# Splitting the last store of a fused conditional-mix and LoRA-expert kernel over two DMA queues

## The reference, cut to what matters

```python
W = weights[condition]                                  # 64 x 32 x 32
y = jnp.einsum('bct,bcd->bdt', x, W)
result = jnp.einsum('bnd,od->bno', y, W_base) + b_base
logits = jnp.einsum('bnd,ed->bne', y, W_gate)
...                                                     # softmax, top 2 of 8, renormalized: route_w
h = jnp.einsum('bnd,erd->bner', y, A)
delta = jnp.einsum('bner,eor->bno', h * route_w[..., None], B)
out = x + result + delta
```

## Time and profile before

| what | us |
|---|---|
| median of three runs | 97.9 |
| lowest and highest of the three | 97.78, 98.39 |
| the profiled execution, its own time | 97.5 |
| span in the profile, first to last instruction | 95.7 |
| granted TensorE clock, mean | 1.00 of full speed |

### The profile page before, as it was taken

How to read it: one execution, slowest core, us unless ns; L and a number is a source line. 1 busy time by engine, 2 the same in 40 slices (tenths; PEclk the granted TensorE clock), 3 DMA queues, 4 the chain that set the end, 5 groups by cost and what they waited for, 6 DMA issues and landing times.

```text
span 95.7 us, 1847 instructions
## 1 busy us (share of the span) xinstructions
PE 90.5 (95%) x657; PEld 87.6 (92%) x657; DVE 65.6 (69%) x234; ACT 23.8 (25%) x56; POOL 16.1 (17%) x29
## 2 busy tenths in 40 slices
PE   5997998999999999999999999999999999999980
PEld 1387997999999999999999999999999999999970
DVE  3768957767586686767675866867676767668880
ACT  5138433130403131221304031311313040311300
POOL 4384303030303021030303030120300000000000
PEclk9999999999999999999999999999999999999999
DMA  0895483060606233140606051331607020302005
GB/s 13 252 335 218 173 265 124 9 219 9 219 7 147 79 132 101 73 153 0 226 7 219 7 188 38 115 115 52 176 8 219 0 110 0 116 0 110 0 10 209
DMA packets 6361, 10.65 MB, mean 111 GB/s; under 512 B 1009, under 2 KB 1617, under 8 KB 6353
## 3 DMA queue, kind: packets, MB, share of 16 engines
q1 hardware_dynamic: 5904, 10.32, 32.6%
q0 software_dynamic: 448, 0.23, 1.1%
HBM read 6.35 MB, written 4.19 MB: 110 GB/s over the span
## 4 chain that ended last, share of the span: by engine, by line
PE 81%; DMA 10%; DVE 2%; issue 1%; ACT 1%; POOL 0%; SPq 0%; DVEq 0%; POOLq 0%
PE main_ps L485 51%; PE y_ps L467 12%; PE main_ps L505 12%; DMA mixw<-cond_w,row_ids 5%; PE main_ps L571 3%; DMA b_raw<-b_lora 3%; DMA table<-cond_w 2%; PE hwT_ps L495 2%; PE y_ps L565 1%; ACT b_hi L297 1%; POOL table_split L238 0%; DVE x_sb L448 0%; SPq L195 0%; DVE hw L385 0%; DVEq L67 0%
## 5 line engine op out<-in xcount | busy, mean ns | idle before, releaser
L485 PE MATMUL main_ps<-w_lo,y_hi 128*128 128x320 f32 x120 | 28.8, 321 | 0.0
L485 PE MATMUL main_ps<-w_hi,y_hi 128*128 128x320 f32 x120 | 28.8, 320 | 0.0
L485 PE MATMUL main_ps<-w_hi,y_lo 128*128 128x320 f32 x120 | 27.4, 311 | 0.0
L242 POOL DMA_INDIRECT mixw<-cond_w,row_ids x14 | 13.7, 976 | 49.3 <-PE y_ps L467 48.6
L485 PEld LDWEIGHTS main_ps<-w_hi,y_lo 128*128 128x128 f32 x120 | 20.3, 188 | 0.0
L485 PEld LDWEIGHTS main_ps<-w_lo,y_hi 128*128 128x128 f32 x120 | 19.9, 189 | 0.1
L485 PEld LDWEIGHTS main_ps<-w_hi,y_hi 128*128 128x128 f32 x120 | 19.4, 190 | 0.0
L467 PE MATMUL y_ps<-mix,x_sb 128*128 128x128 f32 x124 | 16.6, 276 | 0.6 <-DMA x_sb<-x 0.5
L467 PEld LDWEIGHTS y_ps<-mix,x_sb 128*128 128x128 f32 x124 | 15.6, 191 | 0.8 <-issue 0.7
L275 ACT ACTIVATE second<-top 128x1 f32<-128x1 f32 x16 | 4.7, 296 | 44.3 <-DVE top L367 44.3
L407 DVE TENSOR_TENSOR x_sb<-main_ps,x_sb 128x512 f32<-128x512 f32 x15 | 10.4, 691 | 5.7 <-PE main_ps L505 5.7
(11 more groups left out here) (66 smaller groups left out, 77.8 us busy)
## 6 DMA issues: line engine op xcount, KB each, us to landing
x_sb<-x SPq DMA_DIRECT2D x16, 256.0 KB, 2.9
out<-x_sb SPq DMA_DIRECT2D x15, 256.0 KB, 2.0
w_raw<-w_all SPq DMA_DIRECT2D x4, 324.0 KB, 4.6
b_raw<-b_lora SPq DMA_DIRECT2D x1, 256.0 KB, 2.8
bias_sb<-bias SPq DMA_DIRECT2D x1, 256.0 KB, 4.5
out<-x_sb SPq DMA_DIRECT2D x2, 128.0 KB, 1.8
mixw<-cond_w,row_ids POOLq DMA_INDIRECT x14, 2.4
table<-cond_w SPq DMA_DIRECT2D x1, 64.0 KB, 2.0
```

What stands on the lines that cost most here:

```text
L242: pool.indirect_dma_start(mixw[:, t, :], None, cond_w, bass.IndirectOffsetOnAxis(row_ids[:, t:t + 1], 0))\
L485: last = pe.matmul(main_ps[t % 2][:, half, 0:n_cols], y, w[:, half * HALF:half * HALF + n_cols], start=i == 0, stop=i == STEPS - 1)
```

## The change

The left half of the last tile is stored as before. The right half is stored in two DMAs of 64 rows of 1 KB each: partitions 0 to 63 from SyncE's queue, partitions 64 to 127 from ACT's queue, where the wait for `result_ready` and the DMA stand behind ACT's last instruction. The final wait asks for 18 stores in place of 17.

```diff
-            for half in range(2):
-                n = slice(half * BASE, (half + 1) * BASE)
-                sp.wait_ge(result_ready, LAST + half + 1)
-                sp.dma_start(out_tiles[LAST, :, n], x_sb[:, LAST, n]).then_inc(stored, 16)
-            sp.wait_ge(stored, 16 * (TILES + 1))
+            sp.wait_ge(result_ready, LAST + 1)
+            sp.dma_start(out_tiles[LAST, :, 0:BASE], x_sb[:, LAST, 0:BASE]).then_inc(stored, 16)
+            sp.wait_ge(result_ready, LAST + 2)
+            sp.dma_start(out_tiles[LAST, 0:P // 2, BASE:D], x_sb[0:P // 2, LAST, BASE:D]).then_inc(stored, 16)
+            sp.wait_ge(stored, 16 * (TILES + 2))
...
             split_hwT(LAST)
+
+            act.wait_ge(result_ready, LAST + 2)
+            act.dma_start(out_tiles[LAST, P // 2:P, BASE:D], x_sb[P // 2:P, LAST, BASE:D]).then_inc(stored, 16)
```

## The result

The changed kernel took 98.44 us, median of 22 runs (97.73 to 99.3), against 97.83 for 22 runs of the kernel before: a ratio of 1.0062, 95% interval 1.0039 to 1.0084, or 0.38 to 0.82 us more. It is slower by a little over half of one per cent. The forecast was 0.1 us faster. Ratios are formed from the fast runs alone (here all but one of each kernel), and need not be the quotient of the medians that stand beside them.

A forecast was written before the change was run, and what follows sets the result against it. TensorE, busy 95% of the span, was taken to bound the kernel; the change touches only the tail behind it. All parts cost 0 except the filled traffic hole, -0.11 us: median 97.9 to 97.8, range 97.4 to 98.5.

The forecast's parts named there:

- the five steps of the tail: Behind the last addition, for the right half's store: issue 0.45, start of traffic 0.49, traffic 0.50, landing 0.35, engines meeting 0.4 us.
- ACT can issue 0.03 us behind the addition: On ACT's queue: its store follows the second addition by 0.03 us, as SyncE's did the first, at 93.44.
- ACT's issue 0.33: On ACT's queue: the DMA's issue takes 0.33 us, SyncE's shortest, ending at 93.77; traffic could start at 94.26.
- SyncE's half: SyncE's last store, now 64 rows: issued at 93.48 as before, issue kept at 0.45 us, traffic from 94.42.
- The traffic: Last 128 KB on the DMA engines: both halves at the present rate, ending 0.11 us earlier, at 94.82.
- The zero end of my bounds: End of the tail: no gain if a half moves no faster than a whole store (94.42 + 0.50 = 94.92).
- The sign that I had named: Forecast is wrong if, among other signs, traffic of the last 128 KB stretches over more than 0.63 us from 94.30.
- The hole of 0.11 us: DMA engines, 94.30 to 94.55: share 0.56 leaves 0.11 us idle awaiting SyncE's slow issue; ACT's half fills it.
- Rival B: Right half's stores: 64-row halves at half rate, one after the other, 0.50 us each; +0.37 us, median 98.3, chance 0.07.
- Rival A: SyncE's last issue falls with its rows from 0.45 to 0.33; -0.20 us, median 97.7, chance 0.12.
- Rival C: ACT's DMA issue is slow, costing from 0.75 us on; +0.23 to +0.86 us, median 98.1 to 98.8, chance 0.10.
- Rival D: Outside the span, 1.8 us: a third DMA-issuing queue adds 0.9 us, median 98.8, chance 0.05.

## Why the prediction was wrong, point by point

- **Where the kernel is bound, and the five steps of the tail:** right. The same steps carry the account of after, and the last two (0.36, and 0.38 to 0.39) didn't move.
- **ACT can issue 0.03 us behind the addition:** right, 93.24 against 93.21.
- **ACT's issue 0.33:** 0.56 in the changed kernel, but 0.37 with 128 rows. The queue was priced nearly right; the error is that of the next step.
- **SyncE's half, "halving the rows doesn't change that. I keep 0.45":** this is the step that failed first. It measured 0.53 and its first traffic came 0.65 behind, not 0.49 (0.52 by the packets of the kernel before): +0.21 together. I had bounded the issue only downwards (it might fall with the rows), and no row of the trace had a 64-row DMA with which to say that it couldn't rise.
- **The traffic, "If the two halves together move at the rate of now":** the step that failed second. 0.73 us, not 0.50 (0.51 by the packets): +0.21. The overlap was wrong: the halves moved nearly one after the other, at 68 ns a packet in place of 48. The zero end of my bounds, a half no faster than a whole (0.50 for the pair), was still too low. The sign that I had named, over 0.63 us from the point of 94.30, came true: that point, 0.90 us behind the addition, is 94.11 here, and the traffic ended at 95.18.
- **The hole of 0.11 us:** right as a mechanism. It is filled where a second queue issues 128, or 96 and 32, rows. The only kernel whose tail gained as much is the one with the whole right half from ACT (-0.12); in the changed kernel the late first traffic widened the hole instead. ACT's half, which I had at 94.26 and ahead of SyncE's, was not there to fill it: it came 0.29 us behind SyncE's, 0.94 behind the end of its issue in place of 0.49. What sets the order of the two no run shows.
- **Rival B, the halves at half rate and one after the other (+0.37, chance 0.07):** the one whose mechanism came true in part. The whole moved by about its price (+0.42 in the profile), but not by its sum: it had a packet's time doubled, 0.50 for each half, where 0.45 was measured with 0.16 of overlap (0.73 for the pair), and it had nothing for the issue. That its price comes near is in part luck. The rule of the Trainium skill (DMA: Bandwidth & Descriptors, Rules for kernel authors) on two transfers to disjoint partition halves, which I had put beside the sum as one that leaves it at most the hole, should have had the larger chance; the trace agrees that they serialize, with 45 packets of SyncE's half and none of ACT's from 94.45 to 94.70.
- **Rival A** (the issue falls with the rows): with 64 rows it rose, and with 32, 48 and 96 it stayed at 0.45. **Rival C** (ACT slow): 0.37 for 128 rows and 0.56 in the changed kernel, under the 0.75 from which it would have cost; ruled out. **Rival D** (cost outside the span): 1.8 us on both sides; ruled out.
- **The range, 97.4 to 98.5:** it holds the measured 98.44, but at its far end, which stood there for rivals and scatter. The sum itself went the other way, so that is no merit of it.
- **What stays open:** the profiles place 0.42 us and the runs measured 0.61, interval 0.38 to 0.82. The two fit, near its lower end; no run shows where more would lie. Why 64 rows are issued slowly isn't known, nor why two stores of 64 rows issued 0.04 us apart move one after the other.

## What to carry to other kernels

Where the last store of a kernel is on the path, look at how its rows fall before dividing it: in these runs a split at row 64 paid twice, in the issue and in the rate, and a split at row 96, or by columns, cost nothing and brought nothing that could be measured. What a second queue can give is an issue that isn't queued behind another; moving the whole store to the idle queue gave that (0.12 us in the profile; ratio 0.9972, interval 0.9945 to 0.9999, so only just clear of no change), and dividing it wasn't needed. When the trace of before has no row for a shape, give its cost an upper end as well as a lower one.

## What the runs showed of the hardware that I had not expected

- A 64-row store took 0.53 to 0.59 us to issue, on either queue, with rows of 1 KB or 512 bytes, contiguous or every second row. Its traffic began 1.16 to 1.23 us behind the start of SyncE's issue, about 0.2 later than for other stores; 32, 48, 96 and 128 rows behind another issue on SyncE took 0.45.
- An issue on SyncE directly behind another took 0.45, not 0.33; behind an issue on ACT, 0.33 us earlier, it took 0.33.
- Packets of 1 KB from rows 0 to 63 moved at 220 GB/s, from rows 32 to 95 at 307, both with the 16 DMA engines at a share of about 0.9.
- Two stores of 64 rows issued 0.04 us apart from SyncE and ACT moved nearly one after the other. The second one's first packet came 0.28 to 0.29 us behind the first one's; which queue came first differed (SyncE's in the changed kernel, ACT's with even and odd rows).
